# A graph layer's gathers: eight slots in place of four for the gathered node rows

## The chip, the cores and the metric

The kernel runs on one core of a Trainium2 chip. The metric is the device time of one execution in microseconds, given as the median of several runs. The profile is of one execution of its own.

## What is computed

One layer of a graph network over 50000 nodes of 128 features and 25000 edges, all float32:

```python
h = jnp.maximum(_layernorm(x, axis=-1), 0.0)
msg_input = jnp.concatenate([h[src], h[dst], edge_attr], axis=-1)
x1 = jax.nn.relu(msg_input @ Wm1 + bm1)
messages = jax.nn.relu(x1 @ Wm2 + bm2)
agg = jax.ops.segment_sum(messages, dst, num_segments=N)
u = jax.nn.relu(jnp.concatenate([h, agg], axis=-1) @ Wu1 + bu1)
out = x + h + (u @ Wu2 + bu2)
```

The edges are sorted by `dst`. `x1` stands for the first of the two hidden activations.

## The kernel before

The work has two stages, each a block of its own for the five engines.

**The edge stage** (lines 133 to 553) goes through 49 steps. A step takes 512 edges (eight tiles of 128 gathered rows: four of the source nodes, four of the destination nodes) and, beside them, 1024 nodes (eight tiles of consecutive rows). Each engine runs its own program, ordered by hand, one step after another, and they meet through semaphores alone:

- GpSimd (`gpsimd_1`) gathers. For each step it issues eight indirect DMAs (line 261), each of which fetches 128 rows of `x` by the indices in `ends_now`, into a slot of `xg`. There are four slots, a step each. At odd steps it waits first (line 250) until PE has transposed the gathered tiles ("the ends") of step s-3: that frees the slots of steps s-4 and s-3, which steps s and s+1 take. It then waits for gathers of steps s-5 and s-4 to have landed (lines 254, 255) before it copies the next two steps' indices (line 259) over theirs.
- SyncE (`sync_1`) issues the plain DMAs: the loads of 1024 nodes and of the edge attributes (four slots, `xn` and `edge`), and for step s-3 the stores of what the node stage will need, `W_uh h` (`hu_scratch`, line 227) and `x + h` (`xh_scratch`, line 229). In the last steps it already issues the first loads of the node stage into `hu_i` and `xh_i` (lines 216 to 218).
- VectorE (`vector_1`) takes, in the body of step s: the layer norm's small chain for step s-1 (`statistics`, lines 335 to 367, twelve short instructions that depend on each other, with the statistics of the nodes of step s and the sum `x + h` of step s-2 put between them), then the normalising of nine tiles of step s-1 (line 393; the ends in place, in their slot), then the statistics of the ends of step s (line 324), for which it waits until their gathers have landed (line 322).
- ScalarE (`scalar_1`) takes the square root in the middle of VectorE's chain (line 460), the normalising of the other seven tiles (line 444), the ReLU of the transposed blocks into `ht` (line 451), and the evictions of the message network (lines 456, 465, 472, 479).
- PE (`tensor_1`) transposes the sixteen tiles of step s-1 in four blocks (line 504: blocks 0 and 1 are the ends, 2 and 3 the nodes), each block's end counted on `s_tr`, and runs the matmuls of the messages of step s-2 (lines 511 to 534).

The loops are written by `run_steps` (line 30): the first and last steps are laid out straight, the others are a loop whose body holds so many steps that slot numbers are constants: four for VectorE, PE, ScalarE and SyncE, eight for GpSimd.

**The node stage** (lines 556 to 828) goes through 98 groups of 512 nodes: it sums the messages of each node with one-hot matmuls, adds `W_uh h` from `hu_i`, applies the ReLU and `W_out`, adds `x + h` from `xh_i` and stores. `hu_i` and `xh_i`, four slots of 512 columns each, are not used in the edge stage before its last steps.

Of the kernel before, what the change touches and what calls it, by code (L numbers as in the profile page):

```python
# [14 lines left out]
P = 128  # L15
N, E, D, DE = 50000, 25000, 128, 32
W = 4 * P
# [35 lines left out]
def build(nc, x, ends, dst_rows, dst_cols, edge_t, wm1, bm1, wm2, bm2, wu1, bu1, wu2, bu2, out):  # L53
    with ExitStack() as ctx:
# [25 lines left out]
        msgs = sb("msgs", [P, ET + SPARE, D])  # L80
        hu_i, xh_i = sb("hu_i", [P, 4, W]), sb("xh_i", [P, 4, W])

# [10 lines left out]
        s_xn = [sem(f"nodes_loaded{i}") for i in range(4)]  # L93
        s_xg = [sem(f"ends_gathered{i}") for i in range(4)]
        s_cp = sem("ends_copied")
# [37 lines left out]
        with ExitStack() as one:  # L133
# [12 lines left out]

            xg = sb("xg", [P, 4, 8, D], on=one)
            xn = sb("xn", [P, 4, 8, D], on=one)
# [23 lines left out]
            def sync_1(sp):  # L172
# [40 lines left out]
                def body(s, slot, use):  # L213
                    if not below(s, STEPS - 1) and below(s, STEPS + 1):

                        for g in range(2 * (s - STEPS + 1), 2 * (s - STEPS + 2)):
                            load_hu(sp, g, g)
                            load_xh(sp, g, g)
                    if below(s, STEPS - 1) and at_least(s, 3):
                        sp.wait_ge(s_xh, 2 * (s - 2))  # L220
                        sp.wait_ge(s_m1, s - 2)
                        load_nodes(s + 1, (slot + 1) % 4)
                    if at_least(s, 3):
                        to, half = bass.ds(2 * (s - 3), 2), (slot + 1) % 2
                        sp.wait_ge(s_ht, 4 * (s - 2))
                        sp.wait_ge(s_hu, 2 * (s - 2))
                        sp.dma_start(hu_d[to].rearrange("g p f -> p g f"), ht[:, half, 2:4]).then_inc(s_sto[half], 16)
                        sp.wait_ge(s_xh, 2 * (s - 2))
                        sp.dma_start(xh_d[to].rearrange("g p f -> p g f"), xh_o[:, half]).then_inc(s_sto[half], 16)
# [4 lines left out]
            def gpsimd_1(pool):  # L234
# [11 lines left out]
                def body(s, slot8, use8):  # L246
                    slot = slot8 % 4
                    if slot % 2 == 1 and at_least(s, 3):

                        pool.wait_ge(s_tr, 4 * (s - 2) - 2)  # L250

                        pool.wait_ge(s_cp, 4 * use8 + (slot8 + 1) // 2)
                        if at_least(s, 5):
                            pool.wait_ge(s_xg[slot - 1], 128 * (2 * use8 + slot8 // 4))
                            pool.wait_ge(s_xg[slot], 128 * (2 * use8 + slot8 // 4))
                    if slot % 2 == 1 and below(s, STEPS - 3):
                        n = 2 if below(s, STEPS - 4) else 1
                        to = (slot8 + 3) % 8
                        pool.tensor_copy(ends_now[:, to:to + n], ends_all[:, bass.ds(s + 3, n), :]).then_inc(s_cp, 1)  # L259
                    for t in range(8):  # L260
                        pool.indirect_dma_start(  # L261
                            xg[:, slot, t, :], None, x,
                            bass.IndirectOffsetOnAxis(ap=ends_now[:, slot8, t:t + 1], axis=0)).then_inc(s_xg[slot], 16)
                    if not at_least(s, 1):
# [41 lines left out]
            def vector_1(dve):  # L306
# [13 lines left out]

                def stat_of_ends(s, slot, use):
                    dve.wait_ge(s_xg[slot], 128 * use + 128)
                    for t in range(8):
                        ins = dve.bn_stats(bn[:, slot % 2, t, :], xg[:, slot, t, :])
                    ins.then_inc(s_stat, 1)
# [57 lines left out]

                def normalise(s, slot):
                    if at_least(s, 2):
                        dve.wait_ge(s_tr, 4 * (s - 1))
                        dve.wait_ge(s_xs, 2 * (s - 1))
                    for t in range(VECTOR_TILES):
                        if t < 8:
                            of = to = xg[:, slot, t, :]  # L390
                        else:
# [5 lines left out]

                def body(s, slot, use):
                    prev, prev2 = (slot - 1) % 4, (slot - 2) % 4
# [19 lines left out]
                    if at_least(s, 1) and below(s, STEPS + 1):  # L419
                        statistics(s - 1, prev, between)  # L420
                        normalise(s - 1, prev)
                    else:
# [5 lines left out]
                    if below(s, STEPS):  # L428
                        stat_of_ends(s, slot, use)

                run_steps(dve, STEPS + 2, 4, STEPS - 1, 4, body)

# [58 lines left out]
            def tensor_1(pe):  # L491
                pe.wait_ge(s_w, 16 * 11)
                pe.wait_ge(s_cst, 8)

                def transposes(s, slot, qs):
                    for q in qs:
# [5 lines left out]
                        for j in range(4):  # L502
                            of = xg[:, slot, 4 * q + j, :] if q < 2 else zn[:, slot % 2, 4 * (q - 2) + j, :]
                            ins = pe.transpose(p_tr[q][:, j * P:(j + 1) * P], of, ident[:])  # L504
# [32 lines left out]

                def body(s, slot, use):
                    prev, prev2 = (slot - 1) % 4, (slot - 2) % 4
                    for part, qs in enumerate(((), (0, 1), (2, 3))):  # L540
                        if at_least(s, 2):
                            messages(s - 2, prev2, use - (slot < 2), part)
                        if at_least(s, 1) and below(s, STEPS + 1):
                            transposes(s - 1, prev, qs)

                run_steps(pe, STEPS + 2, 4, STEPS - 1, 4, body)

# [312 lines left out]
```

## Time and profile before

| | us |
|---|---|
| median of 3 runs | 1099.22 (1097.98 to 1102.33) |
| the profiled execution | 1093.35 |
| its span, first to last instruction | 1091.5 |
| PE, VectorE, ScalarE, GpSimd busy | 764.7, 701.0, 602.7, 555.8 |
| indirect DMAs issued by GpSimd | 392, 379.5 busy |

Busy times are those of the profiled execution. An engine is busy while an instruction of its datapath runs; waits, branches and the issuing of plain DMAs are not counted. "Idle" before an instruction is the time its engine stood still before it, and the profile names what ended that time: an instruction of another engine whose semaphore came last, "issue" where it sees no wait, "remote" where the semaphore moved but no instruction ended near that moment.

### The profile page before, as it was taken

Reading aid. Unit: us, or ns where it says so; the run is one execution under the profiler, and the core shown is the slowest. Engines: PE = TensorE matmul, PEld = TensorE weight load, DVE = VectorE, ACT = ScalarE, POOL = GpSimd, SP = SyncE. Lnnn points to the kernel's source line nnn. Section 1 sums busy time; section 2 is a strip of 40 time slices with the busy share of each in tenths; the row PEclk is TensorE's granted clock in tenths of the full one; section 3 lists DMA queues with packets and bytes.
Section 4 is the critical chain, followed back from the end, with each engine's and each line's share of the span. In section 5 each row is a group of like instructions: output and inputs, shape, how many; then the busy total and the mean of one; then the engine's idle time right before and its main releaser. Section 6 shows DMA issues by size and latency. Waiting matters only on the chain. (4 is left out here: it accounts for less than half of the span.)

```text
span 1091.5 us, 19557 instructions
## 1 busy us (share of the span) xinstructions
PE 764.7 (70%) x3158; PEld 448.3 (41%) x3159; DVE 701.0 (64%) x2407; ACT 602.7 (55%) x1384; POOL 555.8 (51%) x807
## 2 busy tenths in 40 slices
PE   0375677556559565567776557775598999999998
PEld 0142333322224222233333233332245678877776
DVE  4275466645456555556654556664576999998997
ACT  0163445544445544345554444554484688888886
POOL 7714554434553444555344555443506876665553
PEclk9676788867787778788876788866898999999999
DMA  6234344424344434344443444442451479999999
GB/s 173 53 106 140 99 157 149 151 85 152 105 152 141 134 116 144 111 147 151 147 127 113 135 120 153 150 138 96 135 194 39 128 235 315 328 341 362 356 358 326
DMA packets 99724, 184.54 MB, mean 169 GB/s; under 512 B 15101, under 2 KB 16512, under 8 KB 99700
## 3 DMA queue, kind: packets, MB, share of 16 engines
q1 hardware_dynamic: 87156, 158.57, 42.1%
q0 software_dynamic: 12544, 25.72, 9.7%
q14 instruction: 18, 0.15, 0.1%
q8 instruction: 6, 0.10, 0.0%
HBM read 107.25 MB, written 76.98 MB: 169 GB/s over the span
## 5 line engine op out<-in xcount | busy, mean ns | idle before, releaser
L261 POOL DMA_INDIRECT xg<-x_in,ends_now x392 | 379.5, 968 | 136.1 <-issue 120.7
L451 ACT ACTIVATE ht<-bank 128x512 f32<-128x512 f32 x196 | 108.0, 594 | 202.1 <-remote 160.8
L644 POOL TENSOR_TENSOR low<-msgs,high 128x128 fp32r<-128x128 f32 x303 | 152.9, 522 | 72.5 <-ACT high L724 69.8
L511 PE MATMUL bank<-ht,w_uh 128*128 128x512 f32 x196 | 133.1, 767 | 77.6 <-ACT ht L456 76.2
L520 PE MATMUL bank<-ht,w_src 128*128 128x512 f32 x98 | 69.4, 797 | 168.2 <-ACT ht L451 86.0
L673 DVE TENSOR_SCALAR hot<-node,dst_f,minus_base 128x512 fp32r<-128x512 f32 x229 | 131.0, 615 | 24.3 <-issue 18.3
L777 PE MATMUL bank<-hot,low 128*128 128x512 f32 x303 | 136.3, 450 | 12.8 <-POOL low L644 5.6
L444 ACT ACTIVATE zn<-xn,shift,rstd 128x128 f32<-128x128 f32 x343 | 141.6, 484 | 1.2 <-DVE rstd L363 1.2
L259 POOL COPY ends_now<-ends_all 128x16 int32 (+2 forms) x23 | 4.5, 198 | 258.3 <-PE bank L504 258.3
L352 DVE RECIPROCAL r<-sd 128x16 f32<-128x16 f32 x49 | 12.4, 252 | 184.1 <-ACT sd L460 170.7
L778 PE MATMUL bank<-hot,high 128*128 128x512 f32 x303 | 121.0, 399 | 0.0
L511 PEld LDWEIGHTS bank<-ht,w_uh 128*128 128x128 f32 x196 | 38.0, 229 | 167.2 <-ACT ht L451 88.1
L393 DVE TENSOR_SCALAR xg<-xg,mean,rstd 128x128 f32<-128x128 f32 x392 | 105.6, 345 | 0.0
L811 PEld LDWEIGHTS bank<-w_out,u_t 128*128 128x128 f32 x784 | 99.7, 191 | 13.3 <-issue 6.3
L811 PE MATMUL bank<-w_out,u_t 128*128 128x128 f32 x784 | 104.8, 277 | 0.2 <-ACT u_t L757 0.2
L319 DVE BATCH_NORM_STATS2 bn<-xn 128x6 f32<-128x128 f32 x392 | 98.7, 276 | 0.1
L724 ACT ACTIVATE high<-msgs 128x128 fp32r x303 | 81.9, 299 | 28.0 <-issue 17.0
L520 PEld LDWEIGHTS bank<-ht,w_src 128*128 128x128 f32 x98 | 18.1, 231 | 175.5 <-issue 89.5
L456 ACT ACTIVATE ht<-bank,b_u 128x512 f32<-128x512 f32 x98 | 67.9, 693 | 39.4 <-PE bank L511 37.2
L504 PE MATMUL bank<-ident,xg 128*128 128x128 f32 x392 | 61.4, 290 | 37.7 <-issue 34.4
L527 PE MATMUL bank<-m1t,w_msg 128*128 128x512 f32 x98 | 65.5, 758 | 22.5 <-ACT m1t L465 22.5
L479 ACT ACTIVATE msgs<-bank 128x512 f32 (+1 forms) x49 | 29.1, 593 | 93.3 <-remote 89.6
(77 smaller groups left out, 1274.8 us busy)
## 6 DMA issues: line engine op xcount, KB each, us to landing
hu_scratch<-ht SPq DMA_DIRECT2D x49, 512.0 KB, 2.8
xh_scratch<-xh_o SPq DMA_DIRECT2D x49, 512.0 KB, 3.7
hu_i<-hu_scratch SPq DMA_DIRECT2D x98, 256.0 KB, 4.3
xh_i<-xh_scratch SPq DMA_DIRECT2D x98, 256.0 KB, 4.3
out<-xh_o SPq DMA_DIRECT2D x97, 256.0 KB, 4.3
xn<-x_in SPq DMA_DIRECT2D x48, 512.0 KB
xg<-x_in,ends_now POOLq DMA_INDIRECT x392
edge<-edge_t_in SPq DMA_DIRECT2D x49, 64.0 KB
```

What stands on the lines that cost most here:

```text
L261: pool.indirect_dma_start(xg[:, slot, t, :], None, x, bass.IndirectOffsetOnAxis(ap=ends_now[:, slot8, t:t + 1], axis=0)).then_inc(s_xg[slo ...
L319: dve.bn_stats(bn[:, slot % 2, 8 + t, :], xn[:, slot, t, :])
L393: ins = dve.tensor_scalar(to, of, mean[:, slot % 2, t:t + 1], rstd[:, slot % 2, t:t + 1], ALU.subtract, ALU.mult)
L444: ins = act.activation(zn[:, prev % 2, t - 8, :], xn[:, prev, t - 8, :], ACT.Identity, bias=shift[:, prev % 2, t:t + 1], scale=rstd[:, pre ...
L451: act.activation(ht[:, prev % 2, q, :], p_tr[q][:], ACT.Relu).then_inc(s_ht, 1)
L511: pe.matmul(p_hu[:], w_uh[:], ht[:, slot % 2, 2 + n, :], start=True, stop=True).then_inc(s_hus, 1)
L520: pe.matmul(p_m1[:], w_src[:], ht[:, slot % 2, 0, :], start=True, stop=False)
L644: return pool.tensor_tensor(low[:, at, :], msgs[:, k, :], high[:, at, :].bitcast(F32), ALU.subtract)
L673: return dve.tensor_scalar(hot[:, at, :], node[:], dst_f[:, bass.ds(k, 1)], minus_base[:, bass.ds(g, 1)], ALU.subtract, ALU.is_equal)
L777: pe.matmul(to, low[:, at, :], hot[:, at, :], start=start, stop=False, skip_group_check=True)
L778: return pe.matmul(to, high[:, at, :], hot[:, at, :], start=False, stop=stop, skip_group_check=True)
L811: ins = pe.matmul(to[:, j * D:(j + 1) * D], u_t[:, slot % 2, j * P:(j + 1) * P], w_out[:], start=True, stop=True)
```

## The change

The gathered ends get eight slots. The new slots take no new room in the node stage: `hu_i` and `xh_i` become the halves of one buffer `ring`, and slots 1 to 4 of the gathers lie in it; slots 0 and 5 to 7 lie in `ring_2`, of the size of the old `xg`. GpSimd's wait for the transposes at odd steps now names step s-7 in place of s-3; its waits for landed gathers name the same steps s-5 and s-4 through the new semaphores, of which there is one for each slot. SyncE waits for the transposed ends of step 44 before its first load into `hu_i`. VectorE's and PE's loops have eight steps in their body in place of four.

```diff
--- before.py
+++ after.py
@@ -78,7 +78,9 @@
         minus_base = sb("minus_base", [P, GROUPS])
         ranges = sb("ranges", [1, GROUPS * 2], I32)
         msgs = sb("msgs", [P, ET + SPARE, D])
-        hu_i, xh_i = sb("hu_i", [P, 4, W]), sb("xh_i", [P, 4, W])
+
+        ring = sb("ring", [P, 8, W])
+        hu_i, xh_i = ring[:, 0:4, :], ring[:, 4:8, :]
 
         ht = sb("ht", [P, 2, 4, W])
         xh_o = sb("xh_o", [P, 2, 2, W])
@@ -91,7 +93,7 @@
         s_ext = sem("extremes_moved")
         s_rng = sem("ranges_moved")
         s_xn = [sem(f"nodes_loaded{i}") for i in range(4)]
-        s_xg = [sem(f"ends_gathered{i}") for i in range(4)]
+        s_xg = [sem(f"ends_gathered{i}") for i in range(8)]
         s_cp = sem("ends_copied")
         s_stat = sem("stat")
         s_sd = sem("sd_ready")
@@ -144,7 +146,14 @@
             lo_f, hi_f = sb("lo_f", [GROUPS, 1], on=one), sb("hi_f", [GROUPS, 1], on=one)
             rng_i = sb("rng_i", [GROUPS, 2], I32, on=one)
 
-            xg = sb("xg", [P, 4, 8, D], on=one)
+            ring_2 = sb("ring_2", [P, 8, W], on=one)
+
+            xg = [(ring_2, 0)] + [(ring, 2 * i) for i in range(4)] + [(ring_2, 2 * i) for i in range(1, 4)]
+
+            def ends_of(slot8, t):
+                of, at = xg[slot8]
+                return of[:, at + t // 4, t % 4 * D:(t % 4 + 1) * D]
+
             xn = sb("xn", [P, 4, 8, D], on=one)
             zn = sb("zn", [P, 2, 8, D], on=one)
             edge = sb("edge", [DE, 4, W], on=one)
@@ -214,6 +223,8 @@
                     if not below(s, STEPS - 1) and below(s, STEPS + 1):
 
                         for g in range(2 * (s - STEPS + 1), 2 * (s - STEPS + 2)):
+                            if g == 0:
+                                sp.wait_ge(s_tr, 4 * (STEPS - 5) + 2)
                             load_hu(sp, g, g)
                             load_xh(sp, g, g)
                     if below(s, STEPS - 1) and at_least(s, 3):
@@ -244,23 +255,22 @@
                 pool.wait_ge(s_cp, 1)
 
                 def body(s, slot8, use8):
-                    slot = slot8 % 4
-                    if slot % 2 == 1 and at_least(s, 3):
-
-                        pool.wait_ge(s_tr, 4 * (s - 2) - 2)
-
+                    if slot8 % 2 == 1 and at_least(s, 7):
+
+                        pool.wait_ge(s_tr, 4 * (s - 7) + 2)
+                    if slot8 % 2 == 1 and at_least(s, 3):
                         pool.wait_ge(s_cp, 4 * use8 + (slot8 + 1) // 2)
                         if at_least(s, 5):
-                            pool.wait_ge(s_xg[slot - 1], 128 * (2 * use8 + slot8 // 4))
-                            pool.wait_ge(s_xg[slot], 128 * (2 * use8 + slot8 // 4))
-                    if slot % 2 == 1 and below(s, STEPS - 3):
+                            for back in (5, 4):
+                                pool.wait_ge(s_xg[(slot8 - back) % 8], 128 * (use8 + (slot8 >= back)))
+                    if slot8 % 2 == 1 and below(s, STEPS - 3):
                         n = 2 if below(s, STEPS - 4) else 1
                         to = (slot8 + 3) % 8
                         pool.tensor_copy(ends_now[:, to:to + n], ends_all[:, bass.ds(s + 3, n), :]).then_inc(s_cp, 1)
                     for t in range(8):
                         pool.indirect_dma_start(
-                            xg[:, slot, t, :], None, x,
-                            bass.IndirectOffsetOnAxis(ap=ends_now[:, slot8, t:t + 1], axis=0)).then_inc(s_xg[slot], 16)
+                            ends_of(slot8, t), None, x,
+                            bass.IndirectOffsetOnAxis(ap=ends_now[:, slot8, t:t + 1], axis=0)).then_inc(s_xg[slot8], 16)
                     if not at_least(s, 1):
                         pool.wait_ge(s_cst, 6)
                         pool.affine_select(out=ident[:], in_=ident[:], compare_op=ALU.not_equal, fill=1.0, base=0,
@@ -318,10 +328,10 @@
                 def stat_of_nodes(s, slot, t):
                     dve.bn_stats(bn[:, slot % 2, 8 + t, :], xn[:, slot, t, :])
 
-                def stat_of_ends(s, slot, use):
-                    dve.wait_ge(s_xg[slot], 128 * use + 128)
+                def stat_of_ends(s, slot8, use8):
+                    dve.wait_ge(s_xg[slot8], 128 * use8 + 128)
                     for t in range(8):
-                        ins = dve.bn_stats(bn[:, slot % 2, t, :], xg[:, slot, t, :])
+                        ins = dve.bn_stats(bn[:, slot8 % 2, t, :], ends_of(slot8, t))
                     ins.then_inc(s_stat, 1)
 
                 def statistics(s, slot, between):
@@ -381,13 +391,14 @@
                     dve.tensor_tensor(xh_o[:, slot % 2, h, :], xh_o[:, slot % 2, h, :], b_out[:], ALU.add
                                       ).then_inc(s_xh, 1)
 
-                def normalise(s, slot):
+                def normalise(s, slot8):
+                    slot = slot8 % 4
                     if at_least(s, 2):
                         dve.wait_ge(s_tr, 4 * (s - 1))
                         dve.wait_ge(s_xs, 2 * (s - 1))
                     for t in range(VECTOR_TILES):
                         if t < 8:
-                            of = to = xg[:, slot, t, :]
+                            of = to = ends_of(slot8, t)
                         else:
                             of, to = xn[:, slot, t - 8, :], zn[:, slot % 2, t - 8, :]
                         ins = dve.tensor_scalar(to, of, mean[:, slot % 2, t:t + 1], rstd[:, slot % 2, t:t + 1],
@@ -395,7 +406,8 @@
                         if t in (3, 7, VECTOR_TILES - 1):
                             ins.then_inc(s_zv, 1)
 
-                def body(s, slot, use):
+                def body(s, slot8, use8):
+                    slot, use = slot8 % 4, 2 * use8 + slot8 // 4
                     prev, prev2 = (slot - 1) % 4, (slot - 2) % 4
                     if below(s, STEPS):
 
@@ -418,7 +430,7 @@
 
                     if at_least(s, 1) and below(s, STEPS + 1):
                         statistics(s - 1, prev, between)
-                        normalise(s - 1, prev)
+                        normalise(s - 1, (slot8 - 1) % 8)
                     else:
                         for i in range(12):
                             between(i)
@@ -426,9 +438,9 @@
                         finish_table(dve, did)
                         assert steps[0] == TABLE
                     if below(s, STEPS):
-                        stat_of_ends(s, slot, use)
-
-                run_steps(dve, STEPS + 2, 4, STEPS - 1, 4, body)
+                        stat_of_ends(s, slot8, use8)
+
+                run_steps(dve, STEPS + 2, 8, STEPS - 1, 8, body)
 
             def scalar_1(act):
                 act.wait_ge(s_w, 16 * 11)
@@ -492,7 +504,7 @@
                 pe.wait_ge(s_w, 16 * 11)
                 pe.wait_ge(s_cst, 8)
 
-                def transposes(s, slot, qs):
+                def transposes(s, slot8, qs):
                     for q in qs:
                         pe.wait_ge(s_zv, 3 * s + min(q, 2) + 1)
                         if q >= 2:
@@ -500,7 +512,7 @@
                         if at_least(s, 1):
                             pe.wait_ge(s_ht, 4 * (s - 1) + q + 1)
                         for j in range(4):
-                            of = xg[:, slot, 4 * q + j, :] if q < 2 else zn[:, slot % 2, 4 * (q - 2) + j, :]
+                            of = ends_of(slot8, 4 * q + j) if q < 2 else zn[:, slot8 % 2, 4 * (q - 2) + j, :]
                             ins = pe.transpose(p_tr[q][:, j * P:(j + 1) * P], of, ident[:])
                         ins.then_inc(s_tr, 1)
 
@@ -535,15 +547,16 @@
                                             start=True, stop=True)
                         ins.then_inc(s_msg, 1)
 
-                def body(s, slot, use):
-                    prev, prev2 = (slot - 1) % 4, (slot - 2) % 4
+                def body(s, slot8, use8):
+                    slot, use = slot8 % 4, 2 * use8 + slot8 // 4
+                    prev2 = (slot - 2) % 4
                     for part, qs in enumerate(((), (0, 1), (2, 3))):
                         if at_least(s, 2):
                             messages(s - 2, prev2, use - (slot < 2), part)
                         if at_least(s, 1) and below(s, STEPS + 1):
-                            transposes(s - 1, prev, qs)
-
-                run_steps(pe, STEPS + 2, 4, STEPS - 1, 4, body)
+                            transposes(s - 1, (slot8 - 1) % 8, qs)
+
+                run_steps(pe, STEPS + 2, 8, STEPS - 1, 8, body)
 
             with nc.Block() as block:
                 block.sync(sync_1)
```

## Rows read from the trace of the kernel before

**Rows 1.** The page, part 1: engine, busy us (share of the span), instructions.
```profile
PE 764.7 (70%) x3158; PEld 448.3 (41%) x3159; DVE 701.0 (64%) x2407; ACT 602.7 (55%) x1384; POOL 555.8 (51%) x807
```
**Rows 2.** Busy time by stretch: edge stage, node stage (columns in the first line).
```profile
core 0: us, PE busy (x) PEld busy (x) DVE busy (x) ACT busy (x) POOL busy (x), PEclk, DMA share, GB/s
76.00:812.00 736.00, 481.34 (x1664) 236.08 (x1663) 421.72 (x1830) 363.36 (x785) 344.44 (x373) 0.78 0.42 135
812.00:1091.00 279.00, 259.45 (x1423) 198.88 (x1421) 246.79 (x429) 220.59 (x560) 169.24 (x378) 0.98 0.81 276
```
**Rows 3.** Waits over the span: engine, line, releaser: us, times, longest us.
```profile
POOL ends_now L259 <- PE bank L504: 258.3, 21, 20.6
DVE r L352 <- ACT sd L460: 170.7, 37, 13.3
ACT ht L451 <- remote: 160.8, 29, 11.1
...
POOL xg L261 <- PE bank L504: 15.2, 1, 15.2
```
**Rows 4.** Line 261, the gathers: ns min/median/max, first and last start us.
```profile
L261 POOL DMA_INDIRECT xg<-x_in,ends_now x392: 940/944/1944, 3.9 to 781.4; - x196
```
**Rows 5.** Groups by line, 100 to 780 us: busy us, mean ns, idle before.
```profile
L324 DVE BATCH_NORM_STATS2 bn<-xg 128x6 f32<-128x128 f32 x336 | 68.6, 273 | 0.0
```
**Rows 6.** Timeline of GpSimd, one cycle: start us, us, instruction, idle before.
```profile
392.87 0.94 POOL L261 DMA_INDIRECT xg<-x_in,ends_now  x1 [0.30 <-issue]
...
404.88 0.97 POOL L261 DMA_INDIRECT xg<-x_in,ends_now  x1 [0.48 <-issue]
...
436.08 0.19 POOL L259 COPY ends_now<-ends_all 128x16 int32 x1 [11.17 <-PE bank L504]
```
**Rows 7.** Timeline of the same cycle, PE, VectorE and ScalarE.
```profile
412.53 0.66 PE L504 MATMUL bank<-ident,xg 128*128 128x128 f32 x4 [0.40 <-issue]
412.55 1.64 DVE L324 BATCH_NORM_STATS2 bn<-xg 128x6 f32<-128x128 f32 x8
...
417.10 0.60 ACT L451 ACTIVATE ht<-bank 128x512 f32<-128x512 f32 x1 [3.52 <-remote]
...
425.52 0.60 ACT L451 ACTIVATE ht<-bank 128x512 f32<-128x512 f32 x1 [7.83 <-remote]
...
429.54 0.25 DVE L352 RECIPROCAL r<-sd 128x16 f32<-128x16 f32 x1 [5.35 <-ACT sd L460]
```
**Rows 8.** Busy time by stretch: halves of one burst, and a step behind the last.
```profile
405.00:414.00 9.00, 8.61 (x35) 4.08 (x33) 8.80 (x40) 7.04 (x16) 6.87 (x8) 1.00 0.62 188
414.00:426.00 12.00, 0.95 (x9) 0.71 (x7) 2.30 (x13) 1.08 (x2) 8.47 (x9) 0.71 0.27 83
...
794.00:803.00 9.00, 8.62 (x37) 4.31 (x35) 8.81 (x41) 7.64 (x19) 0.00 (x0) 1.00 0.66 227
```
**Rows 9.** Timeline of the start: VectorE and GpSimd.
```profile
29.59 1.79 DVE L324 BATCH_NORM_STATS2 bn<-xg 128x6 f32<-128x128 f32 x8 [0.17 <-issue]
...
54.34 0.94 POOL L261 DMA_INDIRECT xg<-x_in,ends_now  x1 [0.31 <-issue]
...
59.81 0.18 DVE L360 TENSOR_TENSOR r<-r,veps 128x16 f32<-128x16 f32 x1 [1.71 <-remote]
...
75.90 0.19 POOL L259 COPY ends_now<-ends_all 128x16 int32<-128x16 int32 x1 [20.62 <-PE bank L504]
```
**Rows 10.** Timeline of the end of the edge stage: GpSimd's last burst, VectorE's steps.
```profile
762.27 0.94 POOL L261 DMA_INDIRECT xg<-x_in,ends_now  x1 [15.20 <-PE bank L504]
...
794.24 0.20 DVE L335 TENSOR_TENSOR pair<-bn 128x32 f32<-128x32 f32 x1
...
796.67 0.16 DVE L360 TENSOR_TENSOR r<-r,veps 128x16 f32<-128x16 f32 x1
...
803.40 0.19 DVE L335 TENSOR_TENSOR pair<-bn 128x32 f32<-128x32 f32 x1
```
**Rows 11.** Line 36, the loops' branch on PE's sequencer: ns min/median/max, first and last start us.
```profile
L36 PEldq COMPARE_BRANCH  x33: 76/214/237, 142.6 to 1079.5; - x33
```

## The prediction

> **What bounds the kernel now.** I read the page first: no engine is busy throughout, PE leads with 70% [rows 1]. The table by stage then parts the span: the edge stage from 76 to 812 us holds two thirds of it, with PE busy for 481 of 736 us and GpSimd for 344, while the node stage, 812 to 1091 us, keeps PE busy for 259 of 279 us [rows 2]. The change touches only the edge stage, so the question is who waits there.
>
> The waits [rows 3] name two things. GpSimd waits 258.3 us in 21 stretches, and 15.2 us once more, for the transposes that free its gather slots: 22 waits, 12.4 us each. That is what the change goes after. But VectorE waits 170.7 us for the square root, and ScalarE 160.8 us for transposed blocks, marked "remote": the semaphore moved at a moment when no instruction near it ended.
>
> Is GpSimd's wait on the path? A gather is issued in 944 ns [rows 4], one every 1.25 us (0.94 and 0.30 between) [rows 6], so two steps take 20.0 us, and the stage gives them (762.27 - 75.90) / 21 = 32.7 us [rows 9, 10]. GpSimd is not the bound. The reader of the gathers says the same: VectorE's statistics of the ends, 336 of them in the steady stretch, have 0.0 us of idle time before them [rows 5]. In the cycle shown, the last gather of step 24 is issued at 392.87 us and its step is read at 412.55 us [rows 6, 7]. The gathers are 19 us early with four slots already.
>
> What sets 32.7 us, then? The timeline of one cycle [rows 6, 7]. GpSimd issues 16 gathers from 404.88 to 424.9 us (436.08 less 11.17 idle), then waits until 436.08. In the first 9 us of that burst VectorE is busy for 8.80 of 9.00 us; in the next 12 us VectorE, ScalarE and PE together do almost nothing (2.30, 1.08 and 0.95 us busy), with the DMAs at 0.27 of their time [rows 8]. They aren't out of work: the transposes of the ends are over at 412.53 + 0.66 = 413.2 us, and ScalarE, which only needs their semaphore, takes its blocks at 417.10 and at 425.52 us, 12.3 us after the second was ready [rows 7]. The second comes 0.6 us after GpSimd's last gather. VectorE's reciprocal, due within 2 us of the statistics, runs at 429.54 us. So **releases between the compute engines come late from about 8 us into a burst of gathers until the burst is over**, and in that stretch the step stands nearly still. After the last burst of the kernel a step takes 803.40 - 794.24 = 9.2 us [rows 10], with VectorE as full as in the first part of a burst [rows 8]. A pair of steps is thus 18.3 us of work and 14.4 us of standing still. Why the releases are late the trace does not say; that they go with GpSimd's issuing it shows three times over: in the cycle, at the start and at the end.
>
> **The change, part by part.** *Steady state.* GpSimd waits for the ends of step s-7 and not of step s-3. Both are even steps for the odd s at which it waits, so the wait still ends with an even step's second block of transposes, once in two steps, and lets 16 gathers go. GpSimd still needs 20.0 us of 32.7, so it runs ahead until its eight slots are full and is then held to the pace of the readers, as now. The same burst begins at the same place of the cycle, and the stall in its second half stays. Gain: nothing; at most the 19 us of earliness become 80. I take 0 for the 20 cycles that are left.
>
> *The fill at the start.* Before, GpSimd stops after step 4's gathers, at 54.34 + 0.94 = 55.3 us, and goes on at 75.90 [rows 9]. After, steps 5 to 8 follow at once: 32 gathers by 1.25 us, with their copies 40 us more, to some 95 us; the next wait is for step 2's ends. What do the others do meanwhile? Step 1's statistics of the ends are over at 29.59 + 1.79 = 31.4 us, and VectorE reaches the product of line 360 at 59.81 us, 28.4 us later. In a free step that takes from 794.24 to 796.67 us, and some 0.1 before it: 2.5 us [rows 9, 10]. Progress beside a long burst is 2.5 / 28.4, or 9% of the free pace. I take 10% for the 40 us more: 4 us of work done, **36 us lost**. The bounds are 40 us lost (nothing moves) and 0 (all goes on as in the first 9 us of a burst); I stay near the measured stretch since it is the same burst, only continued.
>
> *The drain at the end.* GpSimd's last burst is released by step 40's ends and not step 44's, so the number of released bursts falls from 22 to 20. Two pairs of steps run free: 2 x (32.7 - 18.3) = **28.8 us gained**. Bounds: 0, if the releases are late for another reason, and 28.8. I take 28.8, since steps 47 and 48 are seen to run so [rows 10].
>
> *The loops.* VectorE and PE turn five times through eight steps where they turned ten times through four. A loop's branch takes PE's sequencer a median of 214 ns [rows 11]; 5 x 0.21 = 1.1 us at most, beside waits longer than it. I take 0. That the row shows the branch, not what comes behind a longer body, leaves both signs open; I put 2 us either way.
>
> *The rest.* SP's new wait, for step 44's ends, stands behind its own wait for step 44's activations of all four blocks, which can only follow those transposes: 0. Behind it are the first loads for the node stage and all later stores; they would move only with it. The semaphores per slot, the other addresses of the buffers, and two waits for landed gathers with the same steps as before: 0, as the readers find the gathers landed [rows 5].
>
> The sum: +36 - 28.8 = **+7 us**. The profiled execution took 1093.35 us (span 1091.5 and 1.85 around it) and would go to about 1100.5. The median of the runs is 1099.22, 5.9 above it, so the forecast for the median is 1106 us.
>
> **A rule weighed.** GpSimd's gathers beside VectorE do not get slower: minimum 940, median 944 ns, maximum 1944 [rows 4]. The Trainium skill, page "SBUF — State Buffer", on the shared port pair, holds that a VectorE operation in a 2-port mode locks GpSimd out, so that it cannot write descriptors. It puts the price of an overlap on GpSimd, and says nothing of PE and ScalarE standing still; by it GpSimd's 12 us of wait per pair would hide everything, and the sum would be 0. The rows speak for another cost, so I sum by the rows and keep 0 as a case.
>
> **The rivals.** *The price is the same everywhere, or nobody's: no change, 1099 us.* The stall then does not follow the burst but sits in every other step whatever GpSimd does. For it: its regularity. Against: the free steps behind the last burst [rows 10]. 13%.
>
> *The fill is cheap, and the drain gains: faster.* The place is the 40 us after 55 us; the deciding point is a progress of 1 - 28.8/40 = 28% of the free pace. VectorE stood mostly behind one late release of ScalarE's in the stretch that I measured; with three engines creeping side by side the pace could be 45%: 22 lost, 28.8 gained, 1092 us. Against it: ScalarE's second block 12 us late, in each long burst. 17%.
>
> *The wait was a bound after all: much faster.* If a deep lead broke the tie between bursts and steps, a pair would fall towards GpSimd's 20.0 us. The price is up to 12.4 us in each of 20 cycles, 250 us; a tenth of it is already 1074. GpSimd's 12 us of slack per pair and idle readers nowhere speak against it. 5%.
>
> *The fill is dearer: slower by more.* PE's releases came the latest, and a step has many; if nothing moves in 40 us, PE's backlog of messages adds to it, and the late releases outlast the burst (they end 4.5 us behind it at the start, 59.8 against 55.3), it is 40 + 5 - 28.8 and up to 10 of backlog: 1115 to 1125 us. 15%.
>
> **How the numbers follow.** The forecast's own case, 1101 to 1111 us, has 50%. What a measurement can tell from no change is about 0.5%, 5.5 us: the line is at 1104.7 us, and a third of my own case lies below it. Slower: 0.33 + 0.15, less a little for the loops, 0.46. No change: 0.17 + 0.13 and some of the cheap fill, 0.33. Faster: 0.21. The range takes in no change, most of the cheap fill and part of the dear one: 1088 to 1119 us.
>
> **What would show it.** Right: GpSimd's first wait begins at 95 us, not 55; step 2's ends are transposed at about 110 us, not 76; 20 waits of 12 us, some 250 us in all; cycles of 32 to 33 us with the same stall in the second half of each burst; a last burst that ends some 65 us before the edge stage does, with steps of 9.2 us behind it; the node stage unchanged at 279 us. Wrong: cycles of another length, a first wait before 90 us, stalls in steps with no gather beside them, or idle time ahead of the statistics of the ends.

## The result and the profile after

The changed kernel takes 1113.3 us (median of 4, 1109.6 to 1117.4) against 1098.6 us: 1.23% slower, 95% interval 0.93% to 1.54%. Forecast was 1106 us, slower, in a range of 1088 to 1119: the time lies in the range, but the change of 14.7 us is twice the 7 that were forecast, and it is 2 us outside the forecast's own case of 1101 to 1111. The profiled execution took 1109.58 us, with a span of 1107.6, 16.1 us longer than before.

GpSimd's first wait and its last burst, from the timeline of GpSimd in the changed kernel:

```profile
94.47 0.95 POOL L271 DMA_INDIRECT ring<-x_in,ends_now  x1 [0.30 <-issue]
115.25 0.20 POOL L269 COPY ends_now<-ends_all 128x16 int32 x1 [19.84 <-PE bank L516]
...
740.00 0.95 POOL L271 DMA_INDIRECT ring<-x_in,ends_now  x1 [14.81 <-PE bank L516]
```

The fill is the 40 us more of gathers that were forecast (95.4 against 55.3 us), and step 2's ends are transposed at 115.25 us in place of 75.90 [rows 9]. From there to the last burst there are 19 cycles of (740.00 - 115.25) / 19 = 32.9 us, against 32.7. The waits, in the list over the span (answering [rows 3]), are 20 in place of 22 (the last of them stands at the gather itself):

```profile
POOL ends_now L269 <- PE bank L516: 234.9, 19, 19.8
ACT ht L463 <- remote: 175.6, 25, 14.1
...
POOL ring L271 <- PE bank L516: 14.8, 1, 14.8
```

One burst in its two parts and a step behind the last burst, by stretch (answering [rows 8], same columns):

```profile
412.00:421.00 9.00, 8.68 (x39) 4.50 (x38) 8.01 (x34) 7.34 (x17) 6.90 (x7) 1.00 0.70 214
421.00:433.00 12.00, 3.22 (x9) 1.06 (x7) 1.67 (x10) 0.73 (x2) 8.51 (x9) 0.75 0.23 64
803.00:812.00 9.00, 8.62 (x36) 4.22 (x35) 8.85 (x40) 7.64 (x18) 0.00 (x0) 1.00 0.64 225
```

The second part of a burst is nearly as dead as before (PE 3.22 us busy in place of 0.95, VectorE 1.67 in place of 2.30). The first instruction of VectorE's small chain in the last steps, timeline:

```profile
802.84 0.20 DVE L345 TENSOR_TENSOR pair<-bn 128x32 f32<-128x32 f32 x1
812.20 0.20 DVE L345 TENSOR_TENSOR pair<-bn 128x32 f32<-128x32 f32 x1
821.20 0.19 DVE L345 TENSOR_TENSOR pair<-bn 128x32 f32<-128x32 f32 x1
```

Steps of 9.0 to 9.4 us, as in [rows 10]; step 48 begins at 821.20 and not at 803.40 us. **The 17.8 us in between add up**: +39.4 at the fill (115.25 - 75.90); +3.7 over the 19 cycles (624.75 us against 19 x 32.68); and from the last burst's first gather to step 48 81.2 us in place of 41.1 and two cycles of 32.68, 106.5 together, so -25.3. Behind step 48 lie 286.4 us, against 288.1: -1.7, and the spans differ by 16.1.

The long burst shows something that the trace before did not. VectorE's statistics of the ends of step 1, eight instructions with no semaphore between them, timeline:

```profile
36.70 0.29 DVE L334 BATCH_NORM_STATS2 bn<-ring 128x6 f32<-128x128 f32 x1 [0.44 <-issue]
38.12 0.29 DVE L334 BATCH_NORM_STATS2 bn<-ring 128x6 f32<-128x128 f32 x1 [1.14 <-issue]
39.54 0.29 DVE L334 BATCH_NORM_STATS2 bn<-ring 128x6 f32<-128x128 f32 x1 [1.12 <-issue]
41.65 0.29 DVE L334 BATCH_NORM_STATS2 bn<-ring 128x6 f32<-128x128 f32 x1 [1.82 <-issue]
```

In [rows 9] the eight ran as one row of 1.79 us. Here they are 0.7, 1.4 or 2.1 us apart, and the gathers 1.25. It is then not the releases alone that come late beside a burst: the engine's own instructions do. They cost something at once: VectorE begins the chain of step 1 at 54.35 us and not at 40.28, so it was 14 us behind before the 40 us of new gathers began. And the late spell outlasts the burst. The last gather ends at 95.42 us, and the statistics of step 2 still come one by one until 101.27; the chain behind them starts at 105.62, 10.2 us after the last gather.

The same is seen in the steady stretch, mostly behind a turn of VectorE's longer loop. Timeline, step 23's chain and step 24's statistics:

```profile
445.76 0.20 DVE L345 TENSOR_TENSOR pair<-bn 128x32 f32<-128x32 f32 x1 [2.48 <-issue]
...
457.09 0.29 DVE L334 BATCH_NORM_STATS2 bn<-ring 128x6 f32<-128x128 f32 x1 [1.13 <-issue]
457.80 0.29 DVE L334 BATCH_NORM_STATS2 bn<-ring 128x6 f32<-128x128 f32 x1 [0.42 <-issue]
459.23 0.29 DVE L334 BATCH_NORM_STATS2 bn<-ring 128x6 f32<-128x128 f32 x1 [1.13 <-issue]
461.37 0.29 DVE L334 BATCH_NORM_STATS2 bn<-ring 128x6 f32<-128x128 f32 x1 [1.84 <-issue]
```

GpSimd was released at 442.78 us, and these statistics start at 453.49, 10.7 us later. In the kernel before, all that stand beside a released burst start 8.0 to 9.1 us after the release, and none is stretched. Of the 392 statistics of the ends, the changed kernel has 40 with such idle time, 34.2 us in all. Whether they are late because they now fall into the burst's second part, or because code is fetched there, this trace does not part; the experiments come back to the turns.

### The profile page after: what moved, and what is told of

The parts are those of the page before. It is cut to its first block and busy times, and to the rows that moved or that the text cites. A ratio compares the mean times of both kernels' runs of the same rounds, so it can differ in the third digit from the quotient of the medians.

```text
span 1107.6 us, 19435 instructions
## 1 busy us (share of the span) xinstructions
PE 761.8 (69%) x3158; PEld 450.2 (41%) x3159; DVE 703.7 (64%) x2407; ACT 602.2 (54%) x1384; POOL 558.2 (50%) x807
## 5 line engine op out<-in xcount | busy, mean ns | idle before, releaser
L271 POOL DMA_INDIRECT ring<-x_in,ends_now x392 | 380.6, 971 | 135.7 <-issue 120.7
L523 PE MATMUL bank<-ht,w_uh 128*128 128x512 f32 x196 | 126.8, 733 | 76.2 <-ACT ht L468 74.4
L516 PE MATMUL bank<-ident,ring 128*128 128x128 f32 x392 | 63.5, 296 | 83.1 <-remote 62.7
L404 DVE TENSOR_SCALAR ring<-ring,mean,rstd 128x128 f32<-128x128 f32 x392 | 106.0, 347 | 2.1 <-issue 2.1
L334 DVE BATCH_NORM_STATS2 bn<-ring 128x6 f32<-128x128 f32 x392 | 83.9, 277 | 34.2 <-issue 34.2
L523 PEld LDWEIGHTS bank<-ht,w_uh 128*128 128x128 f32 x196 | 35.7, 219 | 163.2 <-ACT ht L463 82.8
L516 PEld LDWEIGHTS bank<-ident,ring 128*128 128x128 f32 x392 | 47.6, 151 | 124.7 <-issue 85.7
L345 DVE TENSOR_TENSOR pair<-bn 128x32 f32<-128x32 f32 x49 | 9.7, 197 | 112.4 <-remote 85.7
```

The costliest lines, as they stand in the source:

```text
L271: pool.indirect_dma_start(ends_of(slot8, t), None, x, bass.IndirectOffsetOnAxis(ap=ends_now[:, slot8, t:t + 1], axis=0)).then_inc(s_xg[slo ...
L404: ins = dve.tensor_scalar(to, of, mean[:, slot % 2, t:t + 1], rstd[:, slot % 2, t:t + 1], ALU.subtract, ALU.mult)
L523: pe.matmul(p_hu[:], w_uh[:], ht[:, slot % 2, 2 + n, :], start=True, stop=True).then_inc(s_hus, 1)
```

## The experiments

Two theories stood: the lead costs by its fill and gives back by its drain, beside bursts that hold up the other engines; or the longer loops, the new buffers or the longer straight code cost the 14 us. Each run has the kernel before measured beside it on the same chip, and that turned out to matter most. In the edits, "..." marks lines left out.

**Eight slots, the old wait.**

```diff
-                    if slot8 % 2 == 1 and at_least(s, 7):
-                        pool.wait_ge(s_tr, 4 * (s - 7) + 2)
+                    if slot8 % 2 == 1 and at_least(s, 3):
+                        pool.wait_ge(s_tr, 4 * (s - 3) + 2)
```

> The changed kernel with its eight slots, ring buffer and loops of eight steps kept, but GpSimd waits for the ends of step s-3 again. If the lead is the cause (a fill of 40 us lost, a drain of 27 us gained, each with releases late beside a burst): back to the kernel before, 1094 to 1104 us, first wait of GpSimd near 55 us, 22 waits. If the longer loops, the buffers' places or the longer straight code at the start cost the 14 us: stays at 1110 to 1117 us.

816.65 us, and the kernel before took **813.42 us** on this chip, where it had taken 1098.6: ratio 1.0038 (1.0020 to 1.0057). Neither number was foreseen. The experiments ran on chips 8, 3, 15 and 2. Which one the first measurements ran on is not on record, so where this text says "the first chip", it could also be the occasion.

**Four slots, released step by step** (in the kernel before; the small operation, on two columns of its own, stands between the wait and the gather).

```diff
-                    if slot % 2 == 1 and at_least(s, 3):
-                        pool.wait_ge(s_tr, 4 * (s - 2) - 2)
+                    if at_least(s, 4):
+                        pool.wait_ge(s_tr, 4 * (s - 4) + 2)
+                        pool.wait_ge(s_idle, s - 3)
+                        pool.tensor_tensor(idle[:, 1:2], idle[:, 0:1], idle[:, 0:1], ALU.add).then_inc(s_idle, 1)
+                    if slot % 2 == 1 and at_least(s, 3):
...
```

> The kernel before, four slots, but GpSimd is released step by step: at each step it waits for the ends of step s-4 (eight gathers, 10 us a burst, in place of sixteen, 20 us). If the releases come late only from about 8 us into a burst: the stall of 14 us a pair shrinks to some 2 us a step, steps of 11 to 13 us in place of 16.3, 900 to 980 us in all. If the stall sits in every other step whatever GpSimd does, or grows with the number of gathers issued: 1090 to 1105 us.

820.29 us, ratio 1.0074 (1.0045 to 1.0102): slower by 6.9 us. GpSimd has 45 instructions more, of 0.32 us each by the median; that they are the cause is likely, not shown.

**Eight slots, released step by step** (the same edit with s - 8 and s - 7 in the changed kernel).

> The changed kernel with eight slots, released step by step (ends of step s-8). If the fill of the eight slots costs by its length alone and the steady state follows the length of the bursts: slower than the four slots released step by step by 13 us or more, since the drain gains less where steps are stalled less: 20 to 40 us slower than that run. If the lead helps once bursts are short: as fast or faster than it.

822.31 us, ratio 1.0103 (1.0073 to 1.0133). It is 2.0 us above the four slots, not 20 to 40: no fill of that size is paid here.

**The fill in the middle.**

```diff
-                    if slot8 % 2 == 1 and at_least(s, 7):
-                        pool.wait_ge(s_tr, 4 * (s - 7) + 2)
+                    if slot8 % 2 == 1 and at_least(s, 3):
+                        back = 3 if isinstance(s, int) and s < 15 else 7
+                        pool.wait_ge(s_tr, 4 * (s - back) + 2)
...
-                run_steps(pool, STEPS, 8, STEPS - 4, 8, body)
+                run_steps(pool, STEPS, 16, STEPS - 4, 8, body)
```

> The changed kernel with GpSimd's wait on step s-3 up to step 14 and on step s-7 from step 15: the extra four slots are filled in the middle of the edge stage, in a burst of 48 gathers (60 us) from near 200 us on. If the fill costs because releases are late beside a burst, wherever it stands: 1106 to 1118 us, with the stall of some 50 us seen there. If it costs only at the start (first loads, straight code): 1094 to 1102 us or less, down to 1072 if the drain's 27 us come for nothing.

815.31 us, ratio 1.0017 (1.0000 to 1.0034). It cannot tell the two apart on this chip, for the same reason.

**The changed kernel itself**, unaltered, on that same chip, and at the end on another one:

> The changed kernel itself, unaltered, beside the kernel before on the chip of this call. The first four experiments found the kernel before at 813 us with no late release and GpSimd issuing without a pause. If this call's chip does the same: GpSimd is the bound in both kernels, no fill and no drain to pay, so 811 to 819 us against 813, ratio 1.000 to 1.006, with the longer loops' share in it. If the chip shows the late releases (kernel before near 1099 us): 1108 to 1118 us as before, ratio 1.010 to 1.015.

> The changed kernel unaltered a third time, five rounds. Three chips so far have shown no late releases, and the longer loops alone cost 0 to 0.3%, all parts together 0.1 to 0.5%. If that is all of it: 1 to 4 us slower than the kernel before of this call (812 to 814), ratio 1.001 to 1.005. If this chip has late releases: 1108 to 1118 us, ratio 1.010 to 1.015. If the 0.3% was a chance of one chip: within 1 us.

816.31 against 813.48 us, ratio 1.0031 (1.0011 to 1.0051), and 815.02 against 813.05 us, ratio 1.0026 (1.0008 to 1.0043). On chips where the kernel before takes 813 us the change costs 2 to 3 us, not 14.

**The kernel before, traced.**

> The kernel before itself, unaltered, for a trace of it on the chip of this call. If the chip shows no late releases, as in the calls so far: 811 to 816 us, GpSimd issuing from 4 to about 518 us without one wait of over 1 us for PE, steps of 10.3 to 10.5 us, so the lead of eight slots has nothing to lengthen. If the time of 1099 us is what this program does and the other kernels' neighbours were an exception: 1095 to 1103 us with 22 waits.

813.2 us, on a third chip. Its waits over the span, its GpSimd's only wait for PE among them (columns as in [rows 3]):

```profile
POOL xg L261 <- issue: 115.3, 389, 0.3
...
DVE bn L324 <- DMA xg<-x_in,ends_now: 63.0, 45, 2.8
...
POOL xg L261 <- PE bank L504: 0.3, 1, 0.3
```

and the edge stage by stretch, columns as in [rows 2]:

```profile
60.00:520.00 460.00, 390.97 (x1575) 197.75 (x1573) 398.69 (x1752) 352.56 (x744) 354.31 (x370) 0.99 0.65 207
```

This looks like another kernel. GpSimd all but never waits (0.3 us for PE): it issues gathers without a break, and it **is the bound**; the reader of the gathers, who never waited in [rows 5], waits for them 45 times, 63.0 us. No wait is marked "remote" among its sixty largest, and the other engines are busy for 77 to 87% of the stage where [rows 2] has 49 to 65%. The program is the same, and so is the gathers' issue, a median of 945 ns. Nor were the transfers slower on the first chip. From the page's queues, the time that packets took as a share of 16 engines' span, before and now:

```profile
q1 hardware_dynamic: 87156, 158.57, 42.1%
q1 hardware_dynamic: 87156, 158.57, 55.9%
```

42.1% of 1091.5 us and 55.9% of 812.1 are 460 and 454 us.

**Pauses.** GpSimd waits for its gathers to land before each group of four, from step 5 on, in the kernel before.

```diff
...
                     for t in range(8):
+                        if t % 4 == 0 and at_least(s, 5):
+                            last = slot if t else (slot - 1) % 4
+                            done = 2 * use8 + slot8 // 4 - (1 if t == 0 and slot == 0 else 0)
+                            pool.wait_ge(s_xg[last], 128 * done + (64 if t else 128))
+                            pool.wait_ge(s_idle, 2 * (s - 5) + 1 + (t > 0))
+                            pool.tensor_tensor(idle[:, 1:2], idle[:, 0:1], idle[:, 0:1], ALU.add).then_inc(s_idle, 1)
```

> The kernel before, but GpSimd waits after every four gathers until they have landed, from step 5 on (a pause of 1 to 2 us before each group of four). Where releases are not late and GpSimd is the bound: each pause lengthens the step, 2 x 1.5 us by 44 steps, some 130 us slower, 900 to 960 us against 813. Where releases come late beside a burst: if a pause lets them through, the stall of 14 us a pair shrinks to a few us and the time falls to 900 to 1000 us from 1099; if a pause of that length doesn't help, bursts get longer and it rises to 1120 to 1250 us.

1061.75 us against 813.48, ratio 1.305 (1.298 to 1.312). The direction was right, the size was not. From its waits:

```profile
DVE bn L334 <- DMA xg<-x_in,ends_now: 306.4, 45, 10.0
...
POOL idle L270 <- DMA xg<-x_in,ends_now: 230.3, 88, 5.3
```

A pause lasts 230.3 / 88 = 2.6 us and not 1.5, and some 0.2 us for the new instruction and the restart go with it (248 us over 88 pauses, less the 2.6); VectorE passes on nearly all of it, 243 us more of waiting than in the trace above. That shows GpSimd as the bound by a second way: what is added to it comes out in the time.

The run also settles a rival. On the first chip TensorE's granted clock in the edge stage was 0.78 [rows 2], against 0.99 in the trace above; was the low clock what held the engines up? The steady part of the pause run:

```profile
60.00:700.00 640.00, 420.33 (x1436) 218.80 (x1435) 364.43 (x1600) 313.18 (x682) 326.17 (x416) 0.78 0.42 135
```

It has the same 0.78 with PE as often idle, and among its sixty largest waits not one is marked "remote". Late releases do not follow from the low clock.

**One gather a step** (tiles 1 to 7 of the ends aren't gathered from step 4 on, so the output is not the layer's; the waits for landed gathers count one a step, and the work of the other engines is unchanged).

```diff
-                    for t in range(8):
+                    for t in range(1 if at_least(s, 4) else 8):
...
```

> The kernel before with one gather a step in place of eight from step 4 on (the other seven tiles of the ends are left as they are, so the work of all other engines is the same and the output is not the layer's). If steps free of GpSimd take 9.2 us: 44 steps fewer by the difference to 10.4 us on a chip without late releases, 755 to 775 us against 813; on a chip with late releases the same 755 to 775 us against 1099, since the stall goes with the gathers. If VectorE and PE need more than 9.2 us a step by themselves: 800 us or more, and 1050 or more where releases are late for another reason.

754.0 us against 813.75, ratio 0.9265 (0.9245 to 0.9284). The timeline of VectorE shows the steps:

```profile
430.11 0.20 DVE L335 TENSOR_TENSOR pair<-bn 128x32 f32<-128x32 f32 x1
...
466.80 0.20 DVE L335 TENSOR_TENSOR pair<-bn 128x32 f32<-128x32 f32 x1
```

Four steps in 36.7 us, 9.2 us each: the same free step that [rows 10] and the end of the changed kernel show on the first chip. With next to no gathers this chip and the first agree; they differ in what stands beside a series of gathers.

**The longer loops alone**, in the kernel before: VectorE's and PE's bodies take `slot8, use8`, with `slot, use = slot8 % 4, 2 * use8 + slot8 // 4`, and

```diff
-                run_steps(dve, STEPS + 2, 4, STEPS - 1, 4, body)
+                run_steps(dve, STEPS + 2, 8, STEPS - 1, 8, body)
...
-                run_steps(pe, STEPS + 2, 4, STEPS - 1, 4, body)
+                run_steps(pe, STEPS + 2, 8, STEPS - 1, 8, body)
```

> The kernel before with one part of the change alone: VectorE's and PE's loops have eight steps in their body (four slots, old buffers, old waits). On a chip without late releases the changed kernel was 0.3% slower. If the loops are the cause (one longer stop of VectorE at each turn of its loop, five by 1.7 us, part of it hidden behind GpSimd): 815 to 818 us against 813.4, ratio 1.002 to 1.005, and 35 or more instruction fetches on queue 14 as in the changed kernel, against 18. If ring, semaphores or the wait cost it: 812 to 814 us, ratio under 1.0015. On a chip with late releases (1099 us): 1099 to 1104 us.

814.32 against 813.75 us, ratio 1.0017 (1.0000 to 1.0033): 0 to 2.7 us, less than the whole change's 0.3% by its middle but not clear of it. The queues of the profile's third part tell more: packets, MB, share. The long loops alone:

```profile
q14 instruction: 41, 0.34, 0.1%
```

and the kernel before, as traced on the third chip:

```profile
q14 instruction: 19, 0.15, 0.1%
```

The first instruction of VectorE's chain, over the span of the long loops alone:

```profile
L335 DVE TENSOR_TENSOR pair<-bn x49: 194/196/203, 24.2 to 527.0; 128x32 f32<-128x32 f32 x49
its engine sat idle before it (us, times) until:
  issue: 8.1, 4
```

In the changed kernel, on the same chip, the statistics of the ends of step 39, and then the first instruction of that step's chain, which stands right behind a turn of the loop:

```profile
427.80 1.65 DVE L334 BATCH_NORM_STATS2 bn<-ring 128x6 f32<-128x128 f32 x8 [1.42 <-DMA ring<-x_in,ends_now]
431.20 0.20 DVE L345 TENSOR_TENSOR pair<-bn 128x32 f32<-128x32 f32 x1 [1.75 <-issue]
```

and the same instruction over that kernel's span, then over that of the kernel before (third chip):

```profile
L345 DVE TENSOR_TENSOR pair<-bn x49: 193/196/247, 23.3 to 526.2; 128x32 f32<-128x32 f32 x49
its engine sat idle before it (us, times) until:
  issue: 8.1, 4
```

```profile
L335 DVE TENSOR_TENSOR pair<-bn x49: 194/196/199, 22.5 to 525.9; 128x32 f32<-128x32 f32 x49
its engine sat idle before it (us, times) until:
```

The changed kernel stops there four times, 8.1 us in all, in the chains of steps 15, 23, 31 and 39, once at each of the four turns between its five bodies; the kernel before with long loops alone does the same, and as it was, never. So the stops come from the longer loops and from nothing else of the change. The Trainium skill, page "Runtime: NRT & Kernel Launch", section "Instruction fetch mechanics", holds that a taken branch whose target has left the two pages kept on the engine must fetch it before it can go on. The packets and the stops agree with it. Of the 8.1 us of stops at most 2.7 reach the end; VectorE would have waited for gathers in part of that time.

**Twice more, to meet a chip of the first kind.**

> The four slots released step by step once more, to meet a chip that has the late releases. On such a chip (kernel before near 1099 us): 900 to 1000 us if releases are late only from some 8 us into a burst, 1090 to 1110 us if not. On a chip without them: 819 to 822 us, as the first time.

> Eight slots with the wait on step s-3 once more, for the same purpose. On a chip with late releases: 1097 to 1106 us if the lead costs the change its 14 us there, 1110 to 1118 us if the loops do. On a chip without them: 814 to 818 us.

820.81 us, ratio 1.0101 (1.0077 to 1.0126), and 814.58 us, ratio 1.0025 (1.0009 to 1.0041), beside 812.99 us. The twelve runs fell on four chips, and on each the kernel before took 813 us.

## Why the prediction was right, and where not

**What bounds the kernel: right for the trace of the profile, and for it alone.** The bursts, their dead second parts and the free steps are in the trace after. "From about 8 us into a burst until the burst is over" holds for the cycles only: in the first burst GpSimd issues from 3.9 us on, and VectorE is busy for 8.12 of the 10 us from 20 to 30; and after the long burst the late spell went on for 10 us without a gather, which the prediction had listed as a sign of being wrong. And the step from "the stall goes with GpSimd's issuing" to a property of the program was not earned: in the runs on chips 8, 3, 15 and 2 GpSimd issues all but without waiting for PE and nobody is held up. Issuing gathers is therefore not enough to hold the others up; something of the first chip or of that occasion has to be added. The low clock alone does not do it, and the transfers were not slower; what it is stays open, and no experiment could be made there. Nor was the order of cause and effect there tested other than by its traces: the short bursts, the late fill and the pauses, meant for it, all ran elsewhere.

**Steady state: right.** It was 0; measured +3.7 us over 19 cycles. Single cycles of the kernel before lie between 31.1 and 36.7 us, so that is no difference.

**The fill: mechanism right, size 3.4 us short.** 36 us lost were forecast, 39.4 came. The progress beside the burst was put at 10%; GpSimd's wait behind the 40 us longer burst was 19.84 us in place of 20.62, so in the net 0.8 us was gained in 40, 2%. The bound of 40 was the better value, but not because nothing moved. VectorE did get on beside the burst, from 54.35 us to the statistics of step 2. What took it back lay at the two ends: 14 us behind at the start, and a late spell 10.2 us past the last gather, where it had been 4.5. The prediction left both out of its sum; it had the second in a rival.

**The drain: right.** The last four steps run free, 821.20 - 784.5 = 36.7 us where 36.6 were forecast. The 28.8 us are there; the stretch ahead of them, from the last burst's first gather to the chain of step 44, took 44.5 us where its counterpart took 41.1, 3.4 us more.

**The loops: taken at 0 with 2 us either way; whether that failed is open.** The branch's own 214 ns said nothing of what stands behind a longer body (the kernel before has eleven bodies and ten turns, the changed one five and four). On chip 8 the longer loops stop VectorE four times, and cost 0 to 2.7 us of the whole change's 2 to 3. The first chip's trace shows the stops too, with 41 packets for 18: 2.50, 2.48 and 1.76 us of idle time in the chains of steps 15, 23 and 31. Their price there can't be read. The cycles and the stretch ahead of the last four steps are 7.1 us longer together, which with the fill's 3.4 and the node stage's -1.7 closes the gap from the forecast's 7 to the spans' 16.1, within rounding. But the cycles that hold a turn took 32.1, 33.1, 32.8 and 34.8 us and the others 31.8 to 33.7, and 7.1 us over 20 stretches are within the scatter of single ones.

**The rivals.** "No change" nearly described the runs on chips 8, 3, 15 and 2: nothing to fill, nothing to drain. "The wait was a bound after all" had it upside down: GpSimd is the bound where it does not wait for PE at all. "The fill is dearer" (1115 to 1125 us) came as close to 1113.3 as the forecast's own case: its fill of 40 us was there, while the 5 to 15 us that it added for what comes behind the burst did not show in the net. That the forecast was in its range owes something to the width of the range: the fill, the largest miss that can be told, explains 3.4 of the 9 us between the sum and the spans; the rest lies in the scatter of the cycles.

## What to carry to other kernels

A deeper buffer moves nothing when its producer is already held to its reader's pace; in the first trace it paid a fill once and got back a drain. Where the producer never waits, as on the other chips, it moves nothing either. Before a slot is added, ask whether the reader ever waits; here it had 0.0 us of idle time. And an unrolled loop body has a price that the branch does not show: look at the instruction queue's packets. A version that beats both kernels did not come out of these runs; on the chips of 813 us the shortest way there would be to take gathers off GpSimd: leaving out seven of eight was worth 60 us.

## What was not expected of the hardware

The same program took 1098.6 us in the first measurements and 813 us on chips 8, 3, 15 and 2, each time with all runs within 1% of one another. Whether the first ones ran on a fifth chip is not on record. The difference lies in the edge stage alone: step 48 began at 803.4 us in the one trace and at 525.9 on chip 3, with 288.1 and 286.2 us behind it. In the slow ones, beside a series of gathers, instructions of VectorE that wait for nothing came 0.7 to 2.1 us apart and semaphores of PE were up to 12 us late, though the gathers' issue took a median of 944 ns there and 945 here. Whoever compares two kernels must measure both on one chip and one occasion: otherwise the changed kernel would have looked 26% faster.
